# A graph attention layer on one core: one-hots 64 wide in two column groups, next terms copied by ScalarE, scores in two parts

## The chip, the core and the metric

The kernel runs on one core of a Trainium2 chip. The metric is the device time of one execution in microseconds (us). Engines are named as in the profile: PE is TensorE, DVE VectorE, ACT ScalarE, POOL GpSimd, SP SyncE.

## What is computed

A graph has 3125 nodes with 768 features and 50000 edges sorted by destination. Two residual layers follow each other; the first is a graph convolution (GCN) with two products by 768 x 768 weights, the second, which alone is changed, is graph attention with 12 heads of 64 features:

```
hh  = relu(layernorm(x)).reshape(n, 12, 64)
ft  = einsum('nhd,ed->nhe', hh, W_fc)
e   = leaky_relu(a1[src] + a2[dst], 0.2)          # a1, a2: ft times attn_l, attn_r
ee  = exp(e - segment_max(e, dst)[dst])
agg = segment_sum(ee / segment_sum(ee, dst)[dst] * ft[src], dst)
x   = x + relu(einsum('nhd,ed->nhe', hh, W_res) + agg)
```

## The kernel before, in words

The GCN fills the first 1297 us of the span. The attention part starts there and is a loop over 25 tiles of 128 nodes. With this graph each tile has one visit ("quad"): the edges that end in its 128 nodes, in 16 chunks of 128 edges (4 subtiles of 32 nodes, called units 0 to 3 here, with 4 chunks each) and one shared chunk for what is left over. The last tile has 53 nodes and two units.

For each visit POOL issues 17 indirect gathers (L1243). Each brings 128 rows of 3168 B from `table3` into the ring buffer `ring`: for each head 64 features and a one, and behind them the 12 source terms a1. The ring holds two visits, so the gathers of visit q+2 for a unit wait for `used[s]` of visit q, which PE sets after that unit's products.

DVE builds `hot` (L1555), a bf16 one-hot of each edge's node within its subtile, and ACT casts it to fp32 as `hot_f` (L1344, `cast_hot`). PE transposes `hot` (L1442), ACT copies that out (L1330), and PE makes the scores of the next visit in PSUM (`scores`, L1447): four products from the transposed one-hots (L1454 to L1457), and then five that add the source terms of the gathered rows (L1461). The terms come from the ring by two DVE copies (L1561, L1562, `take_terms`), which wait until all gathers of that visit have landed.

Then ACT makes the leaky part (L1336, `sloped`), DVE takes a running maximum in both directions along the edges (L1613 to L1619) and subtracts it (L1621), PE transposes the result (L1471), and ACT takes the exponentials (L1368 for DVE's units, L1372 for unit 3). DVE multiplies the gathered rows of units 0, 1 and 2 in place with the weights (L1650) and the shared chunk (L1657); ACT does unit 3 in 48 small operations (L1388). PE adds up the weighted rows (L1492; shared chunk L1507): for every chunk four products, one for each column group g of 32 columns. Each has as weights the 32-wide one-hot of the chunk's subtile and streams the 195 columns of three heads. Sums of head group g lie in partitions 32g to 32g+31 of `ps_acc`, with the subtile in the free dimension.

DVE divides the sums by their denominators (L1567 to L1573, `divide`) into `o_g`, and ACT (`lay`, L1354) moves `o_g` into node order in `ps_n` in 16 copies of 32 x 192. PE adds the residual product to it (L1419, `natural`), and DVE finishes the tile (L1579, `finish`), which SP stores (L1277). `divide` of tile j-1, `lay` of j-1 and `finish` of j-2 run in the visit of tile j.

Each engine works through its list in program order. On ACT it is: cast of the one-hots, exponentials, copy of the transposed one-hots, `a2_of`, 48 scalings, `sloped`, `lay`. On PE: transposes of the exponents' scores, transposes of `hot`, `natural`, a small start of the sums (L1483), units 0 to 2, all scores of the next visit, the shared chunk, unit 3. On DVE: units 0 to 2, `take_terms`, shared chunk, `finish`, the one-hot for two visits ahead, the maximum chain, `divide`. `rescale` runs only where a tile has a second visit; no row of the trace comes from it.

## Time and profile before

| | before |
|---|---|
| median of 3 runs | 1899.82 us (1897.61 to 1903.91) |
| profiled execution | 1901.22 us, its span 1899.5 us |
| granted PE clock, mean | 0.881 of full speed |
| PE / PEld / DVE / ACT / POOL busy | 1327.0 / 879.2 / 1123.7 / 716.8 / 1234.5 us |
| 1672.73 to 1694.97, one visit: PE / DVE / ACT / POOL busy | 15.98 / 18.98 / 19.92 / 16.83 us |
| in that visit: clock, DMA share, GB/s | 0.81, 0.97, 350 |

The profiled execution is 1.7 us longer than its span. Busy shares are read for the attention part alone, since only it is changed. PEclk is the granted clock: 1.00 is 2.4 GHz, 0.50 is 1.2 GHz.

### The profile page before, as it was taken

To read this page: it belongs to the slowest core of one execution; us is meant where nothing else is said; L and a number is where in the kernel's file an instruction comes from. 1 tells how busy PE (TensorE), PEld (TensorE's weight loads), DVE (VectorE), ACT (ScalarE), POOL (GpSimd) and SP (SyncE) were. 2 spreads that over 40 slices of the span, in tenths; PEclk is the share of its full clock that TensorE was granted. 3 is DMA by queue.
4 is the path that set the end of the run, shared out by engine and by line. 5 is a ranking of instruction groups with operands and counts; after the bars stand their busy time and mean duration, and the time that the engine had idled before them with its cause. 6 is when DMAs were issued, how large, how long until landed. Compare 5 with 4: busy or idle time off the path is not lost. (4 is left out here: it accounts for less than half of the span.)

```text
span 1899.5 us, 43588 instructions
## 1 busy us (share of the span) xinstructions
PE 1327.0 (70%) x13579; PEld 879.2 (46%) x13580; DVE 1123.7 (59%) x2027; ACT 716.8 (38%) x2184; POOL 1234.5 (65%) x1297
## 2 busy tenths in 40 slices
PE   6426877787877847777777777793566676677665
PEld 6314444444544524444444444492344544444453
DVE  6623454444544525545555555562788888888887
ACT  6600111111111100001000010171688998989885
POOL 3137777777777457777777777204777777777760
PEclk9977898989999978899999899997788878888887
DMA  6589999999999679999999999388999999999992
GB/s 219 208 210 361 331 328 336 333 332 331 335 334 330 230 239 334 330 324 329 323 333 334 330 326 331 140 322 291 314 335 347 348 352 347 345 347 343 357 320 69
DMA packets 139991, 585.22 MB, mean 308 GB/s; under 512 B 30615, under 2 KB 32751, under 8 KB 139945
## 3 DMA queue, kind: packets, MB, share of 16 engines
q0 software_dynamic: 100272, 497.49, 74.3%
q1 hardware_dynamic: 32563, 67.72, 10.1%
q10 hardware_dynamic: 7110, 19.43, 2.9%
q8 instruction: 25, 0.41, 0.1%
q14 instruction: 21, 0.17, 0.0%
HBM read 534.42 MB, written 50.12 MB: 308 GB/s over the span
## 5 line engine op out<-in xcount | busy, mean ns | idle before, releaser
L667 POOL DMA_INDIRECT ring_c<-table,slot_c x834 | 797.0, 956 | 313.6 <-issue 293.9
L1243 POOL DMA_INDIRECT ring<-table,slot x417 | 413.3, 991 | 141.5 <-issue 115.9
L711 ACT ACTIVATE slot_c<-units 128x8 int32 (+1 forms) x104 | 21.7, 210 | 857.9 <-DMA ring_c<-table,slot_c 812.0
L1388 ACT ACTIVATE ring<-ring,weight x1152 | 279.0, 335 | 0.6
L833 DVE TENSOR_TENSOR hots<-iota,units 128x256 f32<-128x256 bf16 x102 | 43.5, 428 | 391.3 <-PE ps_sum0a L779 123.0
L1650 DVE TENSOR_TENSOR ring<-ring,ps_w 128x3120 f32 x72 | 242.7, 3398 | 16.8 <-ACT ps_w L1368 16.5
L1492 PE MATMUL ps_acc<-ring,hot_f 128*32 128x195 f32 x3136 | 179.1, 376 | 86.0 <-DVE ring L1650 84.1
L808 PE MATMUL ps_ya<-weights,sum_ta 128*128 128x512 f32 (+1 forms) x576 | 190.9, 488 | 0.0
L808 PE MATMUL ps_yb<-weights,sum_tb 128*128 128x512 f32 (+1 forms) x576 | 189.7, 486 | 0.0
L1492 PEld LDWEIGHTS ps_acc<-ring,hot_f 128*32 128x32 f32 x3136 | 105.1, 124 | 148.1 <-DVE ring L1650 109.3
L808 PEld LDWEIGHTS ps_ya<-weights,sum_ta 128*128 128x128 f32 x576 | 110.2, 191 | 77.3 <-issue 69.6
L808 PEld LDWEIGHTS ps_yb<-weights,sum_tb 128*128 128x128 f32 x576 | 109.5, 190 | 76.4 <-issue 68.9
L779 PE MATMUL ps_sum0a<-ring_c,hots 128*32 128x192 f32 x1600 | 86.4, 368 | 78.5 <-DMA ring_c<-table,slot_c 78.5
L779 PE MATMUL ps_sum0b<-ring_c,hots 128*32 128x192 f32 x1600 | 84.9, 361 | 70.0 <-DMA ring_c<-table,slot_c 70.0
L779 PE MATMUL ps_sum1b<-ring_c,hots 128*32 128x192 f32 x1536 | 85.5, 373 | 64.2 <-DMA ring_c<-table,slot_c 64.2
L779 PE MATMUL ps_sum1a<-ring_c,hots 128*32 128x192 f32 x1536 | 85.7, 373 | 62.4 <-DMA ring_c<-table,slot_c 62.4
L1354 ACT ACTIVATE ps_n<-o_g 32x192 f32<-32x192 f32 x384 | 124.6, 324 | 7.7 <-DVE nodes L1579 3.6
L779 PEld LDWEIGHTS ps_sum0a<-ring_c,hots 128*32 128x32 f32 x1600 | 57.9, 121 | 104.8 <-issue 75.0
L779 PEld LDWEIGHTS ps_sum0b<-ring_c,hots 128*32 128x32 f32 x1600 | 57.5, 118 | 95.5 <-issue 79.9
L779 PEld LDWEIGHTS ps_sum1b<-ring_c,hots 128*32 128x32 f32 x1536 | 57.0, 122 | 90.5 <-issue 77.3
L779 PEld LDWEIGHTS ps_sum1a<-ring_c,hots 128*32 128x32 f32 x1536 | 56.9, 122 | 88.7 <-issue 79.2
L854 DVE TENSOR_TENSOR ps_sum0a<-ps_sum0a,naturala 32x192 f32<-32x192 f32 x200 | 73.3, 367 | 8.3 <-ACT naturala L739 5.7
(294 smaller groups left out, 1940.2 us busy)
## 6 DMA issues: line engine op xcount, KB each, us to landing
ring_c<-table,slot_c POOLq DMA_INDIRECT x834, 5.4
table<-ft SPq DMA_DIRECT2D x25, 396.0 KB, 2.8
table<-nodes SPq DMA_DIRECT2D x25, 384.0 KB, 3.3
table<-nodes ACTq DMA_DIRECT2D x25, 384.0 KB, 5.3
turned_table<-h_t SPq DMA_DIRECT2D x25, 384.0 KB, 3.0
nodes<-in_x ACTq DMA_DIRECT2D x24, 384.0 KB
turned_g<-turned_table SPq DMA_DIRECT2D x24, 384.0 KB, 6.5
out_x<-nodes SPq DMA_DIRECT2D x24, 384.0 KB
```

Source lines behind the costliest of these rows:

```text
L667: eng.indirect_dma_start(out=ring[:, t * QH + k, :], out_offset=None, in_=table, in_offset=bass.IndirectOffsetOnAxis(ap=slot[t][:, k:k + 1 ...
L711: eng.activation(slot[t][:, :], units[:, ds(q, 1), t * QH:(t + 1) * QH + t].rearrange("p a c -> p (a c)"), ACT.Copy).then_inc(slot_ready[t ...
L779: last = eng.matmul(block_of(par, s, g), hot, rows[:, g * GB:(g + 1) * GB], start=start, stop=True, skip_group_check=True)
L808: last = eng.matmul(product(jj)[:, c0:c0 + n], turned(jj)[:, k, :], w[:, k, c0:c0 + n], start=(k == 0), stop=(k == KB - 1))
L833: eng.tensor_tensor(hots[k][:, :, :].rearrange("p (s c) d -> p s c d", c=CPU), iota0[:, :].unsqueeze(1).unsqueeze(2).to_broadcast([P, 2, C ...
L854: last = eng.tensor_tensor(block_, block_, natural[s * UD:(s + 1) * UD, g * GB:(g + 1) * GB], ALU.add)
L1243: eng.indirect_dma_start(out=ring[:, b * RB + at * FROW:b * RB + (at + 1) * FROW], out_offset=None, in_=table3, in_offset=bass.IndirectOff ...
L1354: last = eng.activation(ps_n[s * UD:(s + 1) * UD, c0:c0 + GN], o[g * UD:(g + 1) * UD, s, :], ACT.Copy)
L1388: last = eng.activation(head, head, ACT.Copy, scale=weight[:, c, h:h + 1])
L1492: last = eng.matmul(acc_of(s, g), hot_f[:, c, s * UD:(s + 1) * UD], ring[:, x0 + g * GW:x0 + (g + 1) * GW], start=False, stop=True, skip_g ...
L1650: eng.tensor_tensor(mine, mine, given_w[:, 0:CPU, s * H:(s + 1) * H].unsqueeze(3).to_broadcast([P, CPU, H, FH]), ALU.mult).then_inc(scaled ...
```

## The change

The four column groups of 32 become two of 64 (`GA = 2`, `AW = 64`). The fp32 one-hot `hot_f` now holds for every chunk three blocks of 32 columns: the subtile's one-hot, a block of zeros that is set once, and the one-hot of its neighbour. `hot_of(s, c)` takes two adjacent blocks, so that a subtile's one-hot stands in the lower or the upper half of 64 columns, with zeros in the other. A chunk now has two products that stream 390 columns of six heads, where it had four of 195. The shared chunk uses `hot_x`, which is 128 wide with no zero half: four products of 390 columns where there were 16 of 195. `ps_acc` takes two whole banks for two half tiles.

`cast_hot` becomes three copies, and stands behind the exponentials. `lay` becomes four copies of 64 x 384. The closing additions of the last tile become two of 64 rows where there were eight of 32. `take_terms` moves from DVE to ACT, where it stands in front of the last 12 of the 48 scalings (and in front of `lay` in the last tile). `scores` is split: the four products of the one-hots come after unit 1, the five of the terms after unit 2. The sizes of `rden`, `lifts`, `head_of` and `o_g` follow.

```diff
+GA = 2
+UA = US // GA
+AW = UA * UD
-            hot_f = sb(st, "hot_f", [P, UC, P])
+            hot_f = sb(st, "hot_f", [P, GA, CPU, 3, UD])
+            hot_x = sb(st, "hot_x", [P, P])
-            def acc_of(s, g):
-                return ps_acc[g * UD:(g + 1) * UD, s * 256:s * 256 + GW]
+            def acc_of(t, g):
+                return ps_acc[g * AW:(g + 1) * AW, t * 512:t * 512 + GW]
+            def hot_of(s, c):
+                return hot_f[:, s // UA, c, s % UA:s % UA + 2, :].rearrange("p x d -> p (x d)")
+                    def take_terms(q):
+                        rows_landed(eng, q, bounds, passed)
+                        given = ring[:, ds(eng.snap(eng.snap(q % 2) * RB), RB)].rearrange("p (c f) -> p c f", f=FROW)[:, :, H * FH:FROW]
+                        eng.activation(terms[:, 0:CPU, :].rearrange("p c (s h) -> p s c h", h=H), given[:, 0:QX, :].rearrange("p (s c) h -> p s c h", c=CPU), ACT.Copy)
+                        eng.activation(terms[:, CPU, :].rearrange("p (s h) -> p s h", h=H), given[:, QX:QC, :].to_broadcast([P, US, H]), ACT.Copy).then_inc(terms_in, 1)
                     def cast_hot(q, j):
...
-                        eng.activation(hot_f[:, :, :].rearrange("p c e -> p (c e)"), hot[:, ds(par, 1), :, :].rearrange("p a c e -> p (a c e)"), ACT.Copy).then_inc(hot_cast, 1)
+                        given = hot[:, ds(par, 1), :, :]
+                        for t in range(GA):
+                            eng.activation(hot_f[:, t, :, 0:3:2, :], given[:, :, 0:CPU, t * AW:(t + 1) * AW].rearrange("p a c (s d) -> p (a c) s d", d=UD), ACT.Copy)
+                        eng.activation(hot_x[:, :], given[:, :, CPU, :].rearrange("p a e -> p (a e)"), ACT.Copy).then_inc(hot_cast, 1)
                     def lay(j):
...
-                        for g in range(US):
-                            for s in range(US):
-                                c0 = g // 2 * 512 + g % 2 * GN
-                                last = eng.activation(ps_n[s * UD:(s + 1) * UD, c0:c0 + GN], o[g * UD:(g + 1) * UD, s, :], ACT.Copy)
+                        for g in range(GA):
+                            for t in range(GA):
+                                last = eng.activation(ps_n[t * AW:(t + 1) * AW, g * 512:g * 512 + GN], o[g * AW:(g + 1) * AW, t, :], ACT.Copy)
                         def follow(q, nth, left):
-                            cast_hot(q, j)
...
                                 eng.activation(weight[:, :, :], ps_e[:, 0:CPU, mine * H:(mine + 1) * H], ACT.Exp).then_inc(own_made, 1)
+                            cast_hot(q, j)
                             turn_hot(q + 1)
...
+                                if c == CPU - 2:
+                                    take_terms(q + 1)
...
-                                    for g in range(US):
-                                        last = eng.matmul(acc_of(s, g), hot_f[:, c, s * UD:(s + 1) * UD], ring[:, x0 + g * GW:x0 + (g + 1) * GW],
+                                    for g in range(GA):
+                                        last = eng.matmul(acc_of(s // UA, g), hot_of(s, c), ring[:, x0 + g * GW:x0 + (g + 1) * GW],
                                                           start=False, stop=True, skip_group_check=True)
...
-                                for s in range(nu):
-                                    for g in range(US):
-                                        last = eng.matmul(acc_of(s, g), hot_f[:, CPU, s * UD:(s + 1) * UD], ring[:, x0 + g * GW:x0 + (g + 1) * GW],
+                                for t in range(-(-nu // UA)):
+                                    for g in range(GA):
+                                        last = eng.matmul(acc_of(t, g), hot_x[:, t * AW:(t + 1) * AW], ring[:, x0 + g * GW:x0 + (g + 1) * GW],
...
                             by_parity(eng, eng.snap(q % 2), first_products)
-                            scores(q + 1)
+                            scores_of_hots(q + 1)
+                            if early_of(j) > 2:
+                                by_parity(eng, eng.snap(q % 2), next_products)
+                            scores_of_terms(q + 1)
                             by_parity(eng, eng.snap(q % 2), other_products)
...
-                                if s == early_of(j) - 1:
-                                    take_terms(q + 1)
...
-                    for g in range(US):
-                        for s in range(LU):
-                            r, c0 = slice(s * UD, (s + 1) * UD), g // 2 * 512 + g % 2 * GN
-                            last = eng.tensor_tensor(ps_s[r, c0:c0 + GN], ps_s[r, c0:c0 + GN], o[g * UD:(g + 1) * UD, s, :], ALU.add)
+                    for g in range(GA):
+                        r, c0 = slice(0, LU * UD), g * 512
+                        last = eng.tensor_tensor(ps_s[r, c0:c0 + GN], ps_s[r, c0:c0 + GN], o[g * AW:g * AW + LU * UD, 0, :], ALU.add)
```

`first_products` is now units 0 and 1, `next_products` unit 2.

## Rows read from the trace of the kernel before

**Rows 1.** Waits of POOL, 1300 to 1870: waiter, releaser, us, times, longest.
```profile
POOL ring L1243 <- issue: 115.9, 371, 0.6
POOL ring L1243 <- PE ps_acc L1492: 13.5, 32, 2.6
```

**Rows 2.** Chain that ended last, one visit: start, us, what.
```profile
1682.93 1.53 PE ps_acc L1492 x32
...
1685.25 0.86 PE ps_s L1457 x2
1686.11 1.11 PE ps_s L1461 x10
...
1687.84 0.31 ACT ps_n L1354
...
1693.63 0.16 ACT hot_f L1344
...
1694.39 0.36 ACT ps_w L1368
...
1694.97 0.12 DVE ring L1650
```

**Rows 3.** Timeline of the same visit: start, us, engine, line, what, idle before.
```profile
1672.73 3.40 DVE L1650 TENSOR_TENSOR ring<-ring,ps_w 128x3120 f32 x1 [0.70 <-ACT ps_w L1368]
...
1676.19 2.83 PE L1492 MATMUL ps_acc<-ring,hot_f 128*32 128x195 f32 x32 [0.84 <-DVE ring L1650]
...
1679.62 2.37 PE L1492 MATMUL ps_acc<-ring,hot_f 128*32 128x195 f32 x32 [0.60 <-DVE ring L1650]
...
1682.93 1.53 PE L1492 MATMUL ps_acc<-ring,hot_f 128*32 128x195 f32 x32 [0.94 <-DVE ring L1650]
...
1683.76 0.26 DVE L1561 COPY terms<-ring 128x192 f32 x1 [0.88 <-DMA ring<-table,slot]
...
1687.13 1.53 PE L1507 MATMUL ps_acc<-ring,hot_f 128*32 128x195 f32 x32
1687.24 0.70 ACT L1336 ACTIVATE top_g<-ps_s 48x640 f32<-48x640 f32 x1 [1.63 <-PE ps_s L1461]
...
1687.84 5.37 ACT L1354 ACTIVATE ps_n<-o_g 32x192 f32<-32x192 f32 x16
...
1692.09 0.82 DVE L1621 TENSOR_TENSOR score<-ps_s,top_g 48x640 f32<-48x640 f32 x1
...
1693.31 0.96 DVE L1573 TENSOR_TENSOR o_g<-ps_acc,rden 128x768 f32<-128x768 f32 x1
```

**Rows 4.** Groups of the second half by form: count, busy us, mean ns.
```profile
L1561 DVE COPY terms<-ring 128x192 f32 x25 | 6.6, 264 | 17.2 <-DMA ring<-table,slot 15.8 <-issue 1.4
...
L1372 ACT ACTIVATE weight<-ps_s 128x48 f32<-128x48 f32 x24 | 4.9, 206 | 0.0
```

**Rows 5.** Stretches: length, PE, PEld, DVE, ACT, POOL busy, PEclk, DMA, GB/s.
```profile
1667.80:1670.80 3.00, 0.00 (x0) 0.01 (x1) 2.90 (x5) 2.90 (x10) 2.48 (x2) 1.00 1.04 425
1672.40:1675.30 2.90, 2.88 (x14) 2.81 (x14) 2.57 (x1) 2.84 (x13) 2.29 (x3) 0.50 1.03 382
1676.19:1679.02 2.83, 2.83 (x32) 1.38 (x32) 2.83 (x2) 2.83 (x13) 2.22 (x3) 0.50 0.99 355
1679.62:1681.20 1.58, 1.58 (x20) 0.99 (x24) 1.58 (x1) 1.58 (x8) 1.03 (x2) 0.50 0.98 353
...
1587.07:1588.57 1.50, 1.50 (x32) 0.94 (x32) 1.50 (x2) 1.50 (x8) 1.20 (x2) 1.00 1.00 365
...
327.30:341.00 13.70, 7.09 (x132) 4.91 (x132) 3.62 (x6) 0.42 (x2) 10.35 (x12) 1.00 0.94 347
```

**Rows 6.** Timeline of POOL, the first gather of the next visit but one.
```profile
1679.87 0.94 POOL L1243 DMA_INDIRECT ring<-table,slot  x1 [0.53 <-issue]
```

**Rows 7.** Timeline of the tail.
```profile
1881.55 1.53 PE L1492 MATMUL ps_acc<-ring,hot_f 128*32 128x195 f32 x32 [0.37 <-DVE ring L1636]
...
1886.17 2.96 DVE L1678 TENSOR_TENSOR ps_s<-ps_s,o_g 32x192 f32<-32x192 f32 x8 [0.57 <-PE ps_s L1527]
```

More of the change, by code:

```diff
@@ L1234, in _ @@
                     eng.wait_ge(g_mask, 1)
-                    for g in range(US):
-                        last = eng.affine_select(out=head_of[:, g, :, :], in_=head_of[:, g, :, :], compare_op=ALU.not_equal, fill=1.0, base=-g * PR,
-                                                 pattern=[[-H, US], [-1, PR]], channel_multiplier=1)
+                    for g in range(GA):
+                        for s in range(UA):
+                            last = eng.affine_select(out=head_of[:, g, s, :, :], in_=head_of[:, g, s, :, :], compare_op=ALU.not_equal, fill=1.0, base=-s * H - g * PR,
+                                                     pattern=[[-UA * H, GA], [-1, PR]], channel_multiplier=1)
                     last.then_inc(g_const, 1)
@@ L1432, in rescale @@
                         eng.sem_inc(passed, 1)
-                        for g in range(US):
-                            last = eng.matmul(ps_l[g * UD:(g + 1) * UD, 64:64 + US * PR], lift[:, :], head_of[:, g, :, :].rearrange("p s k -> p (s k)"), start=True, stop=True)
+                        for g in range(GA):
+                            for s in range(UA):
+                                r0 = g * AW + s * UD
+                                last = eng.matmul(ps_l[r0:r0 + UD, 64:64 + GA * PR], lift[:, :], head_of[:, g, s, :, :].rearrange("p t k -> p (t k)"), start=True, stop=True)
                         last.then_inc(r_all, 1)
@@ L1443, in turn_hot, with scores_of_hots @@
                         last.then_inc(hot_tr, 1)
-                    def scores(q):
+                    def scores_of_hots(q):
                         eng.wait_ge(hot_tc, q + 1)
@@ L1481, in visit @@
                                     eng.sem_inc(passed, 1)
-                                for s in range(0, US, 2):
-                                    eng.matmul(ps_acc[:, s * 256:s * 256 + 2], ident_b[:, :], nil[:, :], start=True, stop=True, skip_group_check=True)
+                                for t in range(GA):
+                                    eng.matmul(ps_acc[:, t * 512:t * 512 + 2], ident_b[:, :], nil[:, :], start=True, stop=True, skip_group_check=True)
                             with eng.Else():
@@ L1496, in first_products, with next_products @@
                             def first_products(b):
-                                for s in range(early_of(j)):
+                                for s in range(min(2, early_of(j))):
+                                    unit(b, s)
+                            def next_products(b):
+                                for s in range(2, early_of(j)):
                                     unit(b, s)
@@ L1504, in other_products @@
                                 x0 = b * RB + QX * FROW
-                                for s in range(nu):
-                                    for g in range(US):
-                                        last = eng.matmul(acc_of(s, g), hot_f[:, CPU, s * UD:(s + 1) * UD], ring[:, x0 + g * GW:x0 + (g + 1) * GW],
+                                for t in range(-(-nu // UA)):
+                                    for g in range(GA):
+                                        last = eng.matmul(acc_of(t, g), hot_x[:, t * AW:(t + 1) * AW], ring[:, x0 + g * GW:x0 + (g + 1) * GW],
                                                           start=False, stop=True, skip_group_check=True)
@@ L1517, in _ @@
                     turn_hot(0, 0)
-                    scores(0)
+                    scores_of_hots(0)
+                    scores_of_terms(0)
                     tiles(eng, step)
@@ L1674, in _ @@
                     eng.wait_ge(o_nat, NT)
-                    for g in range(US):
-                        for s in range(LU):
-                            r, c0 = slice(s * UD, (s + 1) * UD), g // 2 * 512 + g % 2 * GN
-                            last = eng.tensor_tensor(ps_s[r, c0:c0 + GN], ps_s[r, c0:c0 + GN], o[g * UD:(g + 1) * UD, s, :], ALU.add)
+                    for g in range(GA):
+                        r, c0 = slice(0, LU * UD), g * 512
+                        last = eng.tensor_tensor(ps_s[r, c0:c0 + GN], ps_s[r, c0:c0 + GN], o[g * AW:g * AW + LU * UD, 0, :], ALU.add)
                     last.then_inc(o_den, 1)
                     eng.wait_ge(o_den, NT * 2 + 1)
-                    mine = node(NT - 1)[0:LAST].rearrange("p (g x) -> p g x", g=2)
-                    eng.scalar_tensor_tensor(out=mine, in0=ps_s[0:LAST, :].rearrange("p (g x) -> p g x", g=2)[:, :, 0:2 * GN], scalar=0.0, in1=mine, op0=ALU.max, op1=ALU.add).then_inc(o_fin, 1)
+                    mine = node(NT - 1)[0:LAST].rearrange("p (g x) -> p g x", g=GA)
+                    eng.scalar_tensor_tensor(out=mine, in0=ps_s[0:LAST, :].rearrange("p (g x) -> p g x", g=GA)[:, :, 0:GN], scalar=0.0, in1=mine, op0=ALU.max, op1=ALU.add).then_inc(o_fin, 1)
 def kernel(**inputs):
```

44 lines of the change are left out of this document (20 added, 24 removed).

## The prediction

> **What bounds the kernel now.** I read the waits of POOL first, because the DMA share is 0.97 in the attention part and the gathers could be the bound. Nearly all its gaps are the 0.31 us between two issues (115.9 us in 371) [rows 1]. A gather takes 0.95 us, so 17 need 17 x (0.95 + 0.30) = 21.25 us. In each visit one or two gathers are longer, together by some 0.75 us, which makes 22.0; visits follow each other at 22.2. The first gather of a visit starts 0.85 us after PE has ended unit 0 (1679.02 [rows 3], the gather at 1679.87 [rows 6]), with a gap of 0.53 where 0.30 is usual. So POOL is nearly full, and waits 0.2 us per visit for unit 0's products.
>
> Second, the chain of waits over one visit [rows 2]. It runs from unit 2's products (1682.93) over the scores (to 1687.2) and ACT's `lay` to the cast (1693.63), the exponentials (1694.39) and the next L1650 (1694.97). The timeline of the same visit [rows 3] gives the other branch: the maximum chain ends with L1621 at 1692.91 and PE's transposes of it at 1693.5. Both branches meet at the cast. All times below are counted from DVE's start on unit 0, 1672.73. The next one is at 22.24. PE does unit 0 from 3.46 to 6.29, unit 1 from 6.89, unit 2 from 10.20 to 11.73, and the terms' products end at 14.47.
>
> Third, stretches with the granted clock [rows 5]. PE is idle for 3.0 us before the transposes, the clock falls to 0.50, and `natural` and unit 0 run at half speed. Of the 25 first stretches of unit 0, 17 are at 0.50, 7 at 1.00 (1587.07 is one), one is between.
>
> **The change part by part.**
>
> *Products, the added cost.* At the full clock 10 records of 128 columns (five fp32 products) take 1.11 us, two of 512 columns take 0.86 [rows 2]: time goes by columns, four passes at 2.4 GHz (5 x 128 x 4 / 2400 = 1.07; 512 x 4 / 2400 = 0.85), not by records. A unit has 16 products of 195 columns and takes 1.53 us [rows 3]. One after another they would take 16 x 195 x 4 / 2400 = 5.2; over four groups at once 1.30, and 0.2 for the end of the pipe. So four groups do run at once. After the change a unit has 8 products of 390 columns over two groups: 8 x 390 x 4 / 2400 / 2 = 2.6 us, 1.3 more. If two groups of 64 did not overlap it would be 5.2, and if records were what costs, 0.8. The 1.53 us row fits overlap to 0.2 us and the 0.86 row excludes cost by records, so I take 2.6, with 2.7 where the next start counts. That is 5.2 us more PE work per visit. The shared chunk stays at 4 x 390 x 4 / 2400 / 2 = 1.3, near the 1.53 of now. PE goes from 15.98 us busy to about 21 of 22.2, so its slack is gone.
>
> The Trainium skill (TensorE: Matmul & The Clock Gate, "Measured speedup vs the span model") gives 2.38 for three column tiles at once. The trace has 5.2 / 1.53 = 3.4 for four, which is the better measure here.
>
> *Order of the scores.* The four products of the one-hots take 1.65 us (1684.46 to 1686.11 [rows 2]), 1.5 without the start. Now they come after unit 2; then they stand between units 1 and 2, where PE is idle for 1.7 us before unit 2. That would save 1.5 us, but the longer unit 1 eats it. At the full clock: unit 0 from 3.46 to 6.1, unit 1 from 6.89 to 9.6, one-hots to 11.1, unit 2 to 13.8, terms to 14.95. That is 0.5 us later than 14.47. At half clock: unit 0's 2.6 us of work begins at half speed. In the visit shown the clock was still 0.50 five us after unit 0 began (1681.20 [rows 5]) and rose there, since unit 1 took 2.37 and unit 2 took 1.53 [rows 3]; in the visit before it had risen after 3.4. I take 4.3 us at half speed, which does 2.15 of the work: unit 0 ends at 3.46 + 4.3 + 0.45 = 8.2. Then unit 1 to 10.9, one-hots 12.4, unit 2 15.1, terms 16.2: 1.7 us later than now. With 5.2 us at half speed it is 2.2 later.
>
> *Cast behind the exponentials.* The exponentials start 0.76 us earlier, at 20.9 instead of 21.66 (1693.63 to 1694.39 [rows 2]). DVE must also have finished `divide`, which ends at 1694.27 [rows 3], 0.70 before L1650 starts. So 0.65 us of it are gained. The cast now takes three copies. From 0.206 us for 48 elements [rows 4] and 0.74 for 640, an element costs 0.9 ns and a copy 0.16 us to begin: 2 x 0.39 + 0.28 = 1.06 us. It ends about 1 us into the visit, 2.4 before PE's first product: hidden.
>
> *`lay`.* Now 16 x 0.335 = 5.37 us on the chain [rows 2, 3]. Four copies of 384 elements cost 4 x (0.16 + 0.35) = 2.0. The 3.3 us gained do not shorten the visit, since the maximum chain of DVE ends at the same moment (1692.91, transposes to 1693.5). After `lay` goes, that branch alone is left.
>
> *Terms.* DVE loses 0.26 + 0.18 us and a wait of 0.88 for landing [rows 3]. It is idle afterwards until `sloped`, so that is worth nothing. ACT gains two copies of 192 and 48 elements, 0.33 + 0.21 us, and the wait. ACT starts its 48 scalings about 1.1 us later (the cast), reaches the terms at some 11.1 and ends at 14.5. If POOL is later by unit 0's delay, the rows land at some 12.5, which pushes the end of the scalings to 16: behind it is `sloped`, which PE's terms let start at 15.0 to 16.2. So the cover is thin but holds. If it is gone, ACT adds up to 0.5 us. SP's load of the next slots and POOL's queue get nothing new in front of them; `finish` and its store come 0.5 to 1 us earlier.
>
> *Sum.* Full clock: -0.65 + 0.5 = -0.15 per visit, 22.1 us, just over POOL's 22.0. Half clock: -0.65 + 1.7 = +1.05, 23.3 us. Now 17 of 25 visits start unit 0 at half clock. PE's idle time before the transposes shrinks from 3.0 to about 2 us (unit 3 ends at z + 4.0, transposes begin at z + 6, z the end of the terms), so somewhat fewer should: I take 0.65. Then 0.65 x 1.05 - 0.35 x 0.15 = +0.63, over 24 steps from visit to visit +15 us. Head: nothing, everything before the first rows land is covered. Tail: unit 1's products 1.53 become 2.7, the closing eight additions 2.96 [rows 7] become two of 384 elements, 0.96 for 768 elements gives about 0.55 each, so -1.85; with an order of products on PE that is up to 1 later, about 0. Profiled execution: 1901.2 + 15 = 1916; it was 1.4 above the median of the runs, so 1915.
>
> **The rivals.**
>
> *A. The clock holds.* Every visit costs -0.15, or at POOL's pace -0.2: 1899.8 - 4 = 1896. For it: in the GCN, bursts of 1.5 us with gaps of up to 2.4 us keep the clock at 1.00 (327.30 to 341.00 [rows 5]), and the new gap is 2 us. Against: the transposes did not keep it up before, and with them the stretch without products is 3.4 us. The Trainium skill (same page, "HAM oscillation — how this bites in real kernels") has it that short enough gaps between bursts leave the clock up, which is this rival.
>
> *B. PE's work was not what mattered, faster.* If a unit costs no more than now, the one-hots' products hidden and the cast gone give -2 us for the engines, and POOL is left: 22.0, or 21.25 if its long gathers vanish. That is -0.2 to -1.0 x 24 = -5 to -23, middle 1886. The column rates speak against it.
>
> *C. Locked at half clock, slower.* The longer visit makes every unit 0 begin at half speed, and the clock rises late: +1.05 to +1.55 x 24 = +25 to +37, 1931. It decides when the share of half-clock visits goes from 17 in 25 to all.
>
> *D. Groups of 64 do not overlap.* 2.6 us more for each unit: terms end some 8 us later, +7.5 x 24 = +180, 2080. Nothing in the trace shows two groups of 64, so it can't be excluded.
>
> **How the numbers follow.** Forecast 0.50; A 0.20; B 0.10; C 0.17; D 0.03. Differences under 0.3% (5.7 us) are not told from no change. The forecast's own range is 1903 to 1927 (share of half-clock visits 0.35 to 1.0), of which a tenth falls within 0.3%. A is within 0.3% for three quarters and faster for the rest; B is faster but for a fifth. Faster: 0.05 + 0.09 = 0.14, say 0.15. Same: 0.05 + 0.15 + 0.02 = 0.22. Slower: 0.63. The range leaves out most of B and D and the top of C: 1892 to 1935.
>
> **What would show it.** Right: a unit's products at 2.6 to 2.8 us at the full clock (16 records); no `lay` and no cast in the chain of waits, in their place the products of units 1 and 2; `sloped` starting at 15 to 16.3 after L1650's first start instead of 14.5; L1368 right behind the transposes of L1471; visits 22.1 us apart where unit 0 starts at the full clock and 23.3 where not; gaps of POOL before the first gather that grow to 1 us and more. Wrong: a unit of 1.5 us (B) or 5.2 (D), a clock that never falls (A), or an ACT that ends its scalings after PE's terms in every visit.

## The result, and the profile after

The median is 1907.94 us (7 runs, 1901.69 to 1913.67) against 1902.96 us of the kernel before beside it (7 runs, 1897.61 to 1904.87). The ratio is 1.0038, 95% interval 1.0020 to 1.0055: slower by 4 to 10 us, where the sum had +15. The profiled execution took 1913.67 us, the longest of the seven, with a span of 1911.9.

I cut both profiled executions at the same three events. The attention part begins with POOL's first `head_of` instruction; then the first scaling of a unit 0 (L1650 before, L1674 after), the last one 24 visits later, and the end.

| us | before | after | difference |
|---|---|---|---|
| up to the attention part (GCN, unchanged) | 1296.45 | 1299.79 | +3.3, scatter |
| from there to the first unit 0 | 39.72 | 43.29 | **+3.6** |
| 24 visits | 536.49 (22.35 each) | 542.13 (22.59 each) | **+5.6** |
| from the last unit 0 to the end | 26.84 | 26.69 | -0.15 |

The groups of the second half, with line, engine, operation, tile, count | busy, mean ns | idle before and its releasers, to hold beside [rows 2 to 4, 7]:

```profile
L1515 PE MATMUL ps_acc<-ring,hot_f 128*64 128x390 f32 x1568 | 315.8, 521 | 25.8 <-DVE ring L1674 24.4 <-ACT ring L1404 0.6 <-DVE ring L1661 0.3
...
L1369 ACT ACTIVATE ps_n<-o_g 64x384 f32<-64x384 f32 x96 | 46.6, 486 | 2.7 <-DVE nodes L1604 1.8
...
L1348 ACT ACTIVATE terms<-ring 128x192 f32 x25 | 9.0, 362 | 21.9 <-DMA ring<-table,slot 21.1 <-issue 0.8
```

A visit that begins at the full clock, as a timeline (start, us, engine, line, what, idle before). It is 21.89 long:

```profile
1753.18 3.40 DVE L1674 TENSOR_TENSOR ring<-ring,ps_w 128x3120 f32 x1
...
1756.63 2.84 PE L1515 MATMUL ps_acc<-ring,hot_f 128*64 128x390 f32 x16 [1.31 <-DVE ring L1674]
...
1764.64 0.36 ACT L1348 ACTIVATE terms<-ring 128x192 f32 x1 [0.51 <-DMA ring<-table,slot]
...
1766.86 1.15 PE L1484 MATMUL ps_s<-ident,terms 128*48 128x128 f32 x9
...
1768.15 0.70 ACT L1343 ACTIVATE top_g<-ps_s 48x640 f32<-48x640 f32 x1
1768.75 1.98 ACT L1369 ACTIVATE ps_n<-o_g 64x384 f32<-64x384 f32 x4
...
1773.97 0.48 PE L1494 MATMUL ps_s<-ident,score 48*128 48x48 f32 x5 [1.92 <-DVE score L1646]
...
1775.07 3.40 DVE L1674 TENSOR_TENSOR ring<-ring,ps_w 128x3120 f32 x1
```

A unit takes 2.84 us. `sloped` (L1343) starts 14.97 after unit 0's scaling, where it was 14.51. PE's gap before the transposes (L1494) is 1.92, where it was 3.0 [rows 5].

The next two visits show what the mean hides, first one whose unit 0 began at half clock (L1515 at 1664.70), then the one after it, at the full clock:

```profile
1661.25 3.40 DVE L1674 TENSOR_TENSOR ring<-ring,ps_w 128x3120 f32 x1
...
1664.70 7.86 PE L1515 MATMUL ps_acc<-ring,hot_f 128*64 128x390 f32 x32 [0.78 <-DVE ring L1674]
...
1670.77 0.94 POOL L1250 DMA_INDIRECT ring<-table,slot  x1 [2.12 <-PE ps_acc L1515]
...
1677.83 0.70 ACT L1343 ACTIVATE top_g<-ps_s 48x640 f32<-48x640 f32 x1 [1.88 <-PE ps_s L1484]
...
1684.74 3.40 DVE L1674 TENSOR_TENSOR ring<-ring,ps_w 128x3120 f32 x1
...
1698.75 0.36 ACT L1348 ACTIVATE terms<-ring 128x192 f32 x1 [3.06 <-DMA ring<-table,slot]
1699.15 2.97 ACT L1404 ACTIVATE ring<-ring,weight  x12
...
1699.39 1.15 PE L1484 MATMUL ps_s<-ident,terms 128*48 128x128 f32 x9 [0.79 <-ACT terms L1349]
...
1702.02 0.68 ACT L1343 ACTIVATE top_g<-ps_s 48x640 f32<-48x640 f32 x1
```

The first is 23.49 long: PE is late, so POOL stands 2.12 us before it may refill unit 0. The second is longer still, 24.43. Its rows land 3 us late, ACT takes the terms only at 14.0 of the visit, and `sloped` waits for the 12 scalings behind them although PE's products had ended at 1700.65 (nine records are shown, the tenth runs from 1700.38). It starts at 17.3. The chain of waits over the same stretch says it in its own way (start, us, what): PE, then POOL and the landing, and no `lay` and no cast anywhere.

```profile
1664.70 7.86 PE ps_acc L1515 x32
...
1688.20 2.87 PE ps_acc L1515 x16
1691.19 0.94 POOL ring L1250
1692.43 5.75 DMA ring<-table,slot
```

The waits of POOL for the units' products, to hold beside [rows 1], have doubled:

```profile
POOL ring L1250 <- PE ps_acc L1515: 26.9, 44, 5.1
```

The longest, 5.1 us, is the one before the loop's first refill of unit 0 (at 1352.83), behind the late head; in the loop itself they reach 2.1.

Three stretches of after (length; busy of PE, PEld, DVE, ACT, POOL; granted clock; DMA share; GB/s): the first 1.5 us of unit 0 in the half-clock visit and in the full-clock visit shown, and 450 us of visits.

```profile
1664.71:1666.21 1.50, 1.50 (x6) 0.67 (x8) 1.50 (x2) 1.50 (x8) 1.14 (x2) 0.50 1.02 356
1756.64:1758.14 1.50, 1.50 (x10) 0.76 (x12) 1.50 (x2) 1.50 (x8) 1.15 (x2) 1.00 1.08 369
1400.00:1850.00 450.00, 377.12 (x2282) 230.08 (x2280) 371.04 (x301) 346.37 (x1302) 338.51 (x341) 0.92 0.96 346
```

Of 25 such starts nine are at 0.50 or 0.55 (17 at 0.50 before [rows 5]), seven between 0.69 and 0.90, nine at 1.00. Counted from 21.9, the nine low visits are 8.9 us too long together. The visits that follow them are 7.1 too long (1.31, 1.94, 1.14, 2.53, 0.21), and another one 0.53. Then 24 x 21.9 + 8.9 + 7.7 = 542. This split belongs to one execution, and experiment 1 shows how far it scatters.

### The profile page after: what moved, and what is told of

Read it like the earlier page. It is cut to its first block and busy times, and to the rows that moved or that the text cites. A ratio compares the mean times of both kernels' runs of the same rounds, so it can differ in the third digit from the quotient of the medians.

```text
span 1911.9 us, 39119 instructions
## 1 busy us (share of the span) xinstructions
PE 1421.7 (74%) x11423; PEld 902.4 (47%) x11424; DVE 1111.1 (58%) x1970; ACT 655.0 (34%) x1998; POOL 1240.2 (65%) x1297
## 5 line engine op out<-in xcount | busy, mean ns | idle before, releaser
L1515 PE MATMUL ps_acc<-ring,hot_f 128*64 128x390 f32 x1568 | 315.8, 521 | 25.8 <-DVE ring L1674 24.4
L1674 DVE TENSOR_TENSOR ring<-ring,ps_w 128x3120 f32 x72 | 242.6, 3398 | 1.9 <-ACT ps_w L1382 1.9
L1515 PEld LDWEIGHTS ps_acc<-ring,hot_f 128*64 128x64 f32 x1568 | 143.5, 145 | 160.1 <-issue 99.6
L856 DVE TENSOR_TENSOR ps_sum0b<-ps_sum0b,naturalb 32x192 f32<-32x192 f32 x200 | 73.3, 367 | 7.9 <-ACT naturalb L741 5.3
```

The lines of the kernel that those rows point to most:

```text
L856: last = eng.tensor_tensor(block_, block_, natural[s * UD:(s + 1) * UD, g * GB:(g + 1) * GB], ALU.add)
L1515: last = eng.matmul(acc_of(s // UA, g), hot_of(s, c), ring[:, x0 + g * GW:x0 + (g + 1) * GW], start=False, stop=True, skip_group_check=True)
L1674: eng.tensor_tensor(mine, mine, given_w[:, 0:CPU, s * H:(s + 1) * H].unsqueeze(3).to_broadcast([P, CPU, H, FH]), ALU.mult).then_inc(scaled ...
```

## The experiments

Four theories were open: ACT takes the first terms in front of the work that PE waits for (head); DVE's or ACT's order makes the late landing count twice (late visits); the half clock is what starts the late visits; and products of 2.8 us leave PE so full that anything more on it is paid for.

**1. ACT's order in the head alone.**

```
                         tile_quads(eng, j, follow)
-                    take_terms(0)
                     turn_hot(0)
                     a2_of(0)
+                    take_terms(0)
```

> The changed kernel, with the very first copy of the terms on ACT put behind the first copy of the transposed one-hots and a2_of, where the changed kernel has it in front. Theory T: in the trace of the changed kernel the scores of the first visit start only after the rows have landed, so the first L1650 comes 3.6 us later after the start of the attention part than before. This run gives that back: 39.7 us instead of 43.3 from the part's first instruction to the first scaling, and 3.6 us less in time than the changed kernel (some 1904 where that has 1908). Rival R1: all of the loss is in the loop (PE's longer products), and this moves less than 1 us.

Measured: 1904.64 (12 runs) against 1903.36, ratio 1.0006 (0.9989 to 1.0024). From the start of the part to the first unit 0 it is 40.15 instead of 43.29; the 24 visits take 538.9 (after 542.1). The timeline of after's head:

```profile
1329.22 0.36 ACT L1348 ACTIVATE terms<-ring 128x192 f32<-128x192 f32 x1 [32.50 <-DMA ring<-table,slot]
1329.62 0.68 ACT L1337 ACTIVATE hot_t<-ps_s 128x640 f32<-128x640 bf16 x1
...
1331.16 0.63 PE L1475 MATMUL ps_s<-hot_t,a_blk 128*48 128x128 f32 x2 [23.92 <-ACT a_blk L1332]
...
1335.90 0.70 ACT L1343 ACTIVATE top_g<-ps_s 48x640 f32<-48x640 f32 x1 [4.84 <-PE ps_s L1484]
```

and of this kernel's:

```profile
1302.83 0.63 PE L1475 MATMUL ps_s<-hot_t,a_blk 128*48 128x128 f32 x2 [1.65 <-ACT a_blk L1332]
...
1323.67 0.36 ACT L1348 ACTIVATE terms<-ring 128x192 f32<-128x192 f32 x1 [20.95 <-DMA ring<-table,slot]
...
1326.69 0.70 ACT L1343 ACTIVATE top_g<-ps_s 48x640 f32<-48x640 f32 x1 [2.52 <-PE ps_s L1484]
```

In after the copy of the transposed one-hots stands behind a wait of 32.5 us for the first rows, so PE's scores of the one-hots begin only at 1331. Without that they are done 20 us before the rows land. From the terms to `sloped` it is 3.0 us instead of 6.7. The head is shown.

The loop of this kernel is that of after, line for line, so its profile also says how much one execution differs from another: 12 of 25 units begin at 0.50 (after: 9 at 0.50 or 0.55), these visits are 10.4 us too long together, the ones behind them only 2.8 (after: 8.9 and 7.1), and the longest wait of POOL for a unit is 2.1 us.

**2. The terms back on DVE**, as the last work before its maximum chain (the two copies as in the kernel before, behind `next_hot`), the rest as after:

```
-                                if c == CPU - 2:
-                                    take_terms(q + 1)
...
                             eng.wait_ge(hot_cast, q + 1)
                             next_hot(q + 2)
+                            take_terms(q + 1)
```

> The changed kernel with the terms' copies back on DVE, but behind the one-hot of two visits ahead, where DVE is idle. Theory T: in the changed kernel six or seven visits end late (sloped 15.2 to 17.3 us after the first scaling instead of 15.0) because the terms landed late and 12 of ACT's scalings stand between the terms and sloped, 3.4 us from the terms' start to sloped. With DVE the terms' start is followed by sloped 0.5 + 1.2 us later at the earliest. Expected: the head gives 3.6 us back as well, visits after one with a half clock cost up to 1.6 us less each, some 6 in all; 10 us less than the changed kernel, 1898, ratio to before 0.998. Rival R1 (only PE's products and the clock set the visits): nothing in the loop, 3.6 us in the head alone, 1904. Rival R2 (POOL's pace is the bound): visits of 22.0, nothing in the loop either where the clock was full.

Measured: 1904.25 (12 runs), ratio 1.0006 (0.9991 to 1.0021). The head is 39.82; that half of the expectation came. The visits take 544.7, no less than after: the half on the late visits failed. The timeline shows who holds `sloped` now:

```profile
1639.96 0.28 DVE L1583 COPY terms<-ring 128x192 f32 x1 [0.84 <-DMA ring<-table,slot]
...
1642.81 0.70 ACT L1343 ACTIVATE top_g<-ps_s 48x640 f32<-48x640 f32 x1 [2.47 <-DVEq L1629]
```

`sloped` needs two signals: PE's products (the last record ended at 1641.7) and one that DVE's queue gives when it enters the next turn of its loop (L1629), behind the copies of the terms. DVE's last copy ended at 1640.3 and the signal came 2.5 us later. So the late terms now hold `sloped` through DVE's queue instead of ACT's scalings, and nothing was won. ACT's order is not the cause by itself: at the two places tried, late terms cost the same.

**3. PE kept busy in its gap**: after, with eight products of 128 columns into an unused part of PSUM at each visit's end.

```
                             by_parity(eng, eng.snap(q % 2), other_products)
+                            for _ in range(8):
+                                eng.matmul(ps_l[:, 128:256], wres_b[:, :], wres_b[:, :], start=True, stop=True, skip_group_check=True)
...
+                    eng.wait_ge(wres_in, 48)
```

> The changed kernel with eight more products of 128 x 128 (fp32, into an unused part of a PSUM bank) at the end of each visit on PE, in the idle time ahead of the transposes: 1.7 us of work in a gap of 1.9. Theory T: visits that start unit 0 at half clock, and those behind them, make up all of the loop's loss. With the clock kept at 1.00 every visit takes 21.9 us: 24 x 21.9 = 526 us from the first to the last scaling of unit 0, instead of 542; 16 us less than the changed kernel, 1892. Rival R3: the clock is a symptom, the late visits come from the landing of rows (DMA is at 0.97) and stay: 540 us. Rival R4: the products in the gap delay the transposes, and each visit gets up to 0.5 us longer.

Measured: 1911.47 (11 runs), ratio 1.0042 (1.0029 to 1.0055); visits 540.0 (22.50 each). A stretch like those above, and the filler with the transposes behind it:

```profile
1707.38:1708.88 1.50, 1.50 (x10) 0.76 (x12) 1.50 (x2) 1.50 (x8) 1.17 (x2) 1.00 1.08 313
```

```profile
1722.72 2.05 PE L1547 MATMUL ps_l<-wres_b 128*128 128x128 f32 x16
...
1725.22 0.48 PE L1494 MATMUL ps_s<-ident,score 48*128 48x48 f32 x5 [0.45 <-issue]
```

Unit 0 starts at 1.00 in 22 of 25 visits. The twenty visits from the fourth on have `sloped` at 14.98 or 14.99 and a length of 22.36 to 22.44. ACT's waits for the rows, 1400 to 1850, tell the same, after first and then this kernel:

```profile
ACT terms L1348 <- DMA ring<-table,slot: 17.7, 16, 3.1
```

```profile
ACT terms L1348 <- DMA ring<-table,slot: 2.6, 3, 1.7
```

So where the half clock is gone, the late visits are gone. Two things changed at once, though: a visit of 22.4 us also leaves POOL, which needs about 21.9 to 22.0 for its 17 gathers, some 0.4 us of room in each. What shows the link by itself are the waits in after: POOL stands 2.05 and 2.12 us in the half-clock visits that begin at 1480.45 and 1661.25, and the terms of the next visits wait 2.46 and 3.06 us for their rows. How much the room contributed is not shown. The filler itself costs 0.5 us of each visit, because it ends at 1724.77 and DVE had the scores ready at 1724.57 (`<-issue`, not `<-DVE`): what the clock gave back, the filler took. At this place PE has no room for eight more products.

**4. The groups of 64 without the new order** (the short `lay` and the cast in three copies come with them): after with the cast in front of the exponentials, the scores whole behind unit 2, and the terms on DVE as before. In short:

```
                         def follow(q, nth, left):
+                            cast_hot(q, j)
...
-                            scores_of_hots(q + 1)
                             if early_of(j) > 2:
                                 by_parity(eng, eng.snap(q % 2), next_products)
+                            scores_of_hots(q + 1)
                             scores_of_terms(q + 1)
```

> One part of the change alone: two column groups of 64 with the zero half, the short lay, the three copies of the cast; but the cast in front of the exponentials, the scores in one piece behind unit 2, and the terms on DVE behind unit 2, as before. Theory T: units of 2.8 us make the terms' products end at 3.46 + 2.8 ... : unit 2 from 10.2 to 13.0, scores 2.7 more: 15.6 instead of 14.5 at full clock, 16.5 at half. The cast falls into the time that lay has left, so it costs nothing in front: visits of 22.24 - 0.65 + 1.1 = 22.7 at full clock, 23.5 at half; +0.8 x 24 = +19 us on before, 1922. Rival R5 (lay was what bounded the visits and the products cost nothing): 22.0 per visit, 1897. Rival R6 (the split of the scores is worth nothing because PE's idle time was there anyway): same time as the changed kernel, 1908.

Measured: 1916.34 (6 runs), ratio 1.0061 (1.0041 to 1.0081); visits 550.9 (22.95 each), one at the full clock 22.59 with `sloped` at 15.67 (forecast 22.7 and 15.6). Against before the groups of 64 with their short `lay` cost 14 us in the visits. ACT's part behind `sloped` in that visit:

```profile
1561.74 0.70 ACT L1343 ACTIVATE top_g<-ps_s 48x640 f32<-48x640 f32 x1 [2.66 <-PE ps_s L1474]
...
1565.83 0.72 ACT L1353 ACTIVATE hot_f<-hot 128x256 f32 x2 [1.50 <-PE ps_acc L1505]
...
1568.07 0.35 ACT L1377 ACTIVATE ps_w<-ps_s 128x240 f32<-128x240 f32 x1 [1.32 <-PE ps_s L1484]
```

The cast is done at 1566.74, before the maximum chain has ended, so it costs nothing although it stands in front. From `sloped` to the exponentials it is 6.33 us, exactly what it is in after (1768.15 to 1774.48), and 7.15 in the kernel before (1687.24 to 1694.39). With the short `lay` the place of the cast makes no difference. In experiment 5, with the long `lay` and the cast behind, it is 6.62, and 0.25 of that is transposes at half clock. So either edit alone takes nearly all of the 0.82 us, and both together no more.

**5. The order alone**: the kernel before, with the cast behind the exponentials and the scores in two parts; groups of 32, `lay` and terms untouched.

```
                         def follow(q, nth, left):
-                            cast_hot(q, j)
...
                                 eng.activation(weight[:, :, :], ps_e[:, 0:CPU, mine * H:(mine + 1) * H], ACT.Exp).then_inc(own_made, 1)
+                            cast_hot(q, j)
...
-                                for s in range(early_of(j)):
+                                for s in range(min(2, early_of(j))):
                                     unit(b, s)
...
-                            scores(q + 1)
+                            scores_of_hots(q + 1)
+                            if early_of(j) > 2:
+                                by_parity(eng, eng.snap(q % 2), next_products)
+                            scores_of_terms(q + 1)
```

> The kernel before with the cast behind the exponentials and the scores in two parts, four column groups of 32, once more, since the last two calls ran where gathers moved 270 GB/s. If the gathers run at 345 GB/s, Theory T: with units of 1.5 us the one-hots' products fit into PE's idle time, sloped starts at 13.0 instead of 14.5, POOL and the landing of rows set the visits: 21.3 to 21.9, loop 515 to 526 instead of 536, ratio to before 0.991 to 0.995. Rival R2: POOL's pace is 22.0, ratio 0.997. Rival R7: lay (5.37 us behind sloped) still holds the exponentials, so only the 0.65 of the cast and the 1.5 of the scores count, which POOL again cuts. If the gathers are slow: 0.996 to 1.0 as in the two calls before.

Measured: **1892.13** (9 runs, 1888.68 to 1897.17) against 1901.88, ratio **0.9954** (0.9942 to 0.9967): faster than both kernels. One visit of it:

```profile
1687.95 3.40 DVE L1660 TENSOR_TENSOR ring<-ring,ps_w 128x3120 f32 x1 [0.16 <-ACT ps_w L1367]
...
1696.99 1.02 PE L1457 MATMUL ps_s<-hot_t,a_blk 128*48 128x512 f32 x2
1698.15 1.53 PE L1494 MATMUL ps_acc<-ring,hot_f 128*32 128x195 f32 x32
...
1699.19 0.26 DVE L1571 COPY terms<-ring 128x192 f32 x1 [1.10 <-DMA ring<-table,slot]
...
1699.70 1.26 PE L1463 MATMUL ps_s<-ident,terms 128*48 128x128 f32 x10
...
1702.60 0.70 ACT L1336 ACTIVATE top_g<-ps_s 48x640 f32<-48x640 f32 x1 [1.00 <-DVEq L1617]
...
1708.41 0.73 PE L1473 MATMUL ps_s<-ident,score 48*128 48x48 f32 x5 [4.67 <-DVE score L1631]
...
1709.80 3.40 DVE L1660 TENSOR_TENSOR ring<-ring,ps_w 128x3120 f32 x1 [0.17 <-ACT ps_w L1367]
```

and POOL's waits over its attention part, to hold beside [rows 1]:

```profile
POOL ring L1243 <- issue: 114.2, 375, 0.3
POOL ring L1243 <- PE ps_acc L1494: 11.8, 30, 1.6
```

A visit takes 21.85 here and 22.03 in the mean (528.7 for 24). DVE waits 0.16 where it waited 0.70 [rows 3]. PE had the terms' scores ready at 1700.96, and `sloped` starts 1.6 later: DVE still has the shared chunk, `finish` and the next one-hot in front of its signal, to 1702.04, and began them late by the landing (1.10). `sloped` waits for that signal in 21 of the visits. Over 20 visits the pace is 22.01, the 22.0 that the prediction gave POOL, and nearly all of POOL's gaps are the 0.3 us of an issue: what is left is the pace of the gathers, and DVE's order behind the landing. The pace is no fixed number: over the four visits of after from 1753.18 to 1840.76 POOL has no gap over 0.31 us and needs 21.9, with one long gather in each.

The clock is not as the prediction had it. PE's gap before the transposes is 4.67 us, longer than the 3.07 of before, and the transposes themselves run at half clock (0.73 us instead of 0.48). Yet only 9 of 25 units 0 begin at 0.50, five lie between 0.57 and 0.69, five between 0.81 and 0.93, six are at 1.00. The length of that gap alone does not set the share.

The runs below were made where the gathers of the unchanged GCN moved less. The record numbers the chips: experiments 1 to 4 ran on chip 8 and experiment 5 on chip 5, but 6, 7, 9 and 10 on chip 0, and 8, 11 and 12 on chip 11. One row each, 100 to 600 us, of the kernel before at the usual rate and of experiment 6:

```profile
100.00:600.00 500.00, 360.86 (x3405) 219.16 (x3406) 214.45 (x517) 63.21 (x111) 362.52 (x382) 0.89 0.94 325
```

```profile
100.00:600.00 500.00, 374.33 (x2769) 198.65 (x2770) 171.29 (x412) 49.12 (x88) 298.11 (x315) 0.82 0.82 271
```

The kernel before takes 2288.59 us beside experiments 6, 7, 9 and 10, 2313.15 beside 8 and 11, and 2289.46 beside 12. They are another regime, and it is not one of late rows: from 1600 to 1860 the terms of experiment 6 never wait for a landing. There PE's own products start late, with gaps that nothing in the profile explains:

```profile
PE ps_acc L1492 <- issue: 49.9, 81, 1.8
```

In the kernel before at the usual rate PE has no such wait for these products in the same stretch. POOL waits for PE, so the gathers slow down with it. These runs say how the orders stand in that regime, not what they do at the usual rate.

**6. The cast alone** on the kernel before, and **7, 8. the order alone** (the kernel of 5), there:

```
-                            cast_hot(q, j)
                             with eng.If(nth < 1):
                                 eng.sem_inc(r_exp, 1)
...
                                 eng.activation(weight[:, :, :], ps_e[:, 0:CPU, mine * H:(mine + 1) * H], ACT.Exp).then_inc(own_made, 1)
+                            cast_hot(q, j)
                             turn_hot(q + 1)
```

> The kernel before with the one-hots' cast behind the exponentials, nothing else. Theory T: the cast gives back up to 0.65 us of the 22.24 in front of L1650; POOL then is the next bound. In the changed kernel stretches of visits follow each other at 21.90 with no wait of POOL, so POOL's pace is at most that: visits of 21.6 to 21.9, loop 520 to 528 instead of 536, ratio 0.995. Rival R2 (POOL's pace is 22.0 to 22.2 and the gain is lost there): loop 530 and more, ratio 0.998 to 1.0, POOL waits vanish. Rival R7: lay, which keeps its 5.37 us, ends with the maximum chain and keeps the exponentials where they were: no gain at all.

> The kernel before with the cast behind the exponentials and the scores in two parts (after unit 1 and after unit 2), with four column groups of 32 and all else as before. Theory T: with units of 1.5 us PE's idle time between units 1 and 2 does hold the one-hots' products, the terms' products end at 13.0 instead of 14.5 and the engines alone would need 20.1 to 20.7 us a visit; so POOL's pace or the landing of the rows sets the visits: 21.3 to 21.9, loop 515 to 526, ratio 0.991 to 0.995. Rival R2: POOL's pace is 22.0: same as the run with the cast alone.

> The kernel before with the cast behind the exponentials and the scores in two parts, four column groups of 32: again, for the same reason. If the gathers run at 345 GB/s: Theory T: the engines' loop is 20.1 to 20.7 us, POOL and the landing of rows set the visits: 21.3 to 21.9, loop 515 to 526, ratio 0.991 to 0.995. Rival R2: POOL's pace is 22.0 and nothing is gained over 0.997. If the gathers are slow again: 0.996 as there.

Measured: the cast alone 2286.02 (12 runs), 0.9994 (0.9980 to 1.0007); the order 2279.40 (10 runs), 0.9958 (0.9945 to 0.9971), and beside 2313.15 it is 2311.49 (12 runs), 0.9985 (0.9970 to 0.9999). So the order is ahead in all three comparisons, by 0.4 to 0.5% in two and by 0.15% in the third, where the interval almost reaches 1. That the cast alone is worth nothing there does not say what it is worth at the usual rate; this stays open.

**9. DVE's scalings of units 1 and 2 left out**, to see POOL's own pace:

```
+                                if s > 0:
+                                    eng.tensor_copy(rows[:, s * CPU, 0, :], rows[:, s * CPU, 0, :]).then_inc(scaled[s], 1)
```

> The kernel before, with DVE's scaling of units 1 and 2 left out (one small copy in its place), so the weights of these two units are missing from the result. The engines' loop gets 6.7 us shorter, and the visits show the pace of POOL and the DMA alone. Theory T: 17 gathers of 1.25 us and 0.3 to 0.8 us of longer ones: 21.5 to 21.9 us a visit. Rival R2: 22.0 or more. If nothing but the issue counts: 21.3.

Measured: one run, 2298.28 beside 2288.59; visits of 28 to 30 us. Inconclusive: where a visit is that long, 22.0 can't be seen. Kernel 5 answered it.

**10 to 12. Experiment 1 with a filler of five products** instead of eight:

```
+                            for _ in range(5):
+                                eng.matmul(ps_l[:, 128:256], wres_b[:, :], wres_b[:, :], start=True, stop=True, skip_group_check=True)
```

> The changed kernel with five instead of eight products of 128 x 128 in PE's gap at the end of a visit (1.3 us, where eight took 2.05 and pushed the transposes 0.5 us back), and with the first copy of the terms behind a2_of. Theory T: the clock stays at 1.00 and nothing is pushed: 21.9 a visit from the fourth on, loop 527 to 530 instead of 542, the head 3.6 us shorter: 1889 to 1893 where the changed kernel has 1908, ratio to before 0.994. Rival R8: 1.3 us of work is too little to keep the clock, visits at half clock come back: 1900 and more. Rival R2: at full clock POOL holds the visits at 22.0 to 22.2: 1896.

> The same kernel as the last one, again, because in the call before the kernel before itself took 2289 us, with gathers that moved 270 instead of 345 GB/s. If the gathers run at 345 GB/s: Theory T as before: the clock stays at 1.00, visits of 21.9, loop 527 to 530, ratio to before 0.994. Rival R8: the clock is not kept, 1900 and more. Rival R2: POOL at 22.0 to 22.2, ratio 0.997. If the gathers are slow again: PE's later end of unit 0 stands in the loop from a row's use to the next gather, so about 1.02 as there.

> The changed kernel with five products of 128 x 128 in PE's gap at the end of a visit and the first copy of the terms behind a2_of, once more, where gathers run at 345 GB/s if the last call's do. Theory T: eight of them kept sloped at 14.98 in all visits but cost 0.5 us each; five (1.3 us) leave the transposes alone: visits of 21.9 to 22.0 (POOL's pace was 22.0 in the last run), loop 528 to 531 instead of 542, and the head 3.6 us shorter: ratio to before 0.995. Rival R8: 1.3 us is too little to keep the clock; some visits of 22.4 to 24 remain, ratio 1.000 as with the first terms moved alone.

Measured, each time where gathers are slower: 2343.03 (6 runs), 1.0243 (1.0213 to 1.0273); 2380.76 (6 runs), 1.0264 (1.0225 to 1.0304); 2361.05 (4 runs), 1.0305 (1.0263 to 1.0346). The 64-wide products with a filler cost 2.4 to 3% there. POOL's waits in the first of them, 1300 to 1880:

```profile
POOL ring L1250 <- PE ps_acc L1515: 70.3, 13, 11.7
```

The rows are not late here either: from 1600 to 1860 ACT never waits for them before it takes the terms (10.0 us in after). PE is: the five filler products, 1.3 us by the expectation, are spread from 1691.87 to 1698.73 in one visit, with gaps `<- issue` of up to 2.5 us. How much of the loss is the filler's and how much the wide groups' was not separated, and whether five products pay at the usual rate stays open.

## Why the prediction was right

The edits of the change come apart as a square of four kernels, by the length of the 24 visits in the profiled execution:

| us for 24 visits | groups of 32 | groups of 64 |
|---|---|---|
| cast first, scores whole, terms on DVE | 536.5 (before) | 550.9 (4) |
| cast behind, scores split | 528.7 (5, terms on DVE) | 542.1 (after), 544.7 (2, terms on DVE) |

By rows the wide groups cost 14.4 us in the old order and 13.5 in the new one (16.0 where the terms are on DVE in both); by columns the new order gains 7.8 with groups of 32 and 8.8 with groups of 64 (6.2 with the terms on DVE). Each cell is one execution, and the same loop gave 542.1 and 538.9 in two of them, so differences of 3 us are not told apart. The ratios of the times say the same: 1.0061 for the groups in the old order, 0.9954 for the order alone. What is left of the two together is small: with the head mended (experiment 1) the ratio to before is 1.0006, 0.9989 to 1.0024, no difference. The direction of the prediction therefore hangs on the head as well.

*The number: right in part by luck.* Counted from a visit of 22.24 us, the sum and the profile compare like this:

| us | forecast | measured |
|---|---|---|
| full-clock gain, 24 visits | 24 x -0.15 = -3.6 | 24 x (21.9 - 22.24) = -8.2 |
| half clock, above a full-clock visit | 0.65 x 24 x 1.2 = +18.7 | +8.9 |
| late visits | 0 | +7.7 |
| irregular visits of before itself | 0 | 24 x 22.24 - 536.5 = -2.7 |
| head | 0 | +3.6 |
| tail | 0 | -0.15 |
| together | +15 | +9 |

Without the two terms that the prediction put at nothing, late visits and head, this gives -2 us, which would not have been told from no change. The half clock was costed at twice what it took, and that covered for both. So the range was met by errors that partly cancel; the mechanisms below are right one by one only where it says so.

*Products: right.* Forecast 2.6 to 2.7 us for a unit, measured 2.84. Two groups of 64 do overlap, so rival D falls; time goes by columns, so B falls.

The Trainium skill (TensorE: Matmul & The Clock Gate, "Measured speedup vs the span model") gives 2.38 for three tiles at once. By 8 products of 390 columns in four passes at 2.4 GHz, 5.2 us one after another, two groups gain 5.2 / 2.84 = 1.83; the 3.4 of four groups stands in the prediction.

*Order of the scores and the cast: right at the full clock.* `sloped` at 14.97 to 14.98, forecast 14.95. The visit is 21.9, forecast 22.1. The sum gave only 0.15 of the two edits' gain after the wider units; 0.34 came: `sloped` is 0.47 later, and the stretch behind it 0.82 shorter where the cast had been given 0.65. With groups of 32 it came down to POOL's pace, 22.0.

*`lay`: price right, role wrong.* Four copies take 1.98 (forecast 2.0), and in after nothing more is gained from them, since DVE's maximum chain holds the transposes until 1773.97. But the prediction let both branches meet at the cast. The cast does not wait for the maximum chain, as experiment 4 shows, where it runs while the chain is still at work; in the kernel before the cast came late because ACT was at `lay` until 1693.2. So what was put down to the moved cast could be had by the short `lay` alone.

*Half clock: mechanism right, share mis-sized.* In the visit shown `sloped` starts at 16.6 (forecast 16.2) and the visit takes 23.5 (forecast 23.3). Over the nine such visits the mean is 22.9. But the share is 9 of 25, 0.36, where I took 0.65. This is the term that made the sum too large. PE's gap before the transposes went from 3.07 to 1.92, as forecast, but that this is why the share fell is not shown: kernel 5 has 9 of 25 as well, with a gap of 4.67, and experiment 1, with 1.92, has 12. Rival A ("the clock holds") is half true, C did not come.

The Trainium skill (the same page, "HAM oscillation — how this bites in real kernels") has it that long enough gaps in PE's work between bursts bring the clock down. Experiment 3 agrees: with 2.05 us of products in the gap, 22 of 25 units begin at 1.00.

*Late visits: a term that I did not have.* The prediction named the growing waits of POOL (1.0 to 2.1 us measured) and then cost only the visit in which they stand. The rows that they delay are the next visit's, and that one is up to 2.5 us longer although PE is at the full clock: 7.1 us in all here, 2.8 in the same loop of experiment 1. "The cover is thin but holds", with up to 0.5 us if it does not, failed here: `sloped` is held for 1.4 us behind ACT's scalings (PE done at 1700.65, `sloped` at 1702.02).

*Head: the step that failed.* "Nothing, everything before the first rows land is covered" counted what the change makes PE and ACT do, not the order in which ACT does it. A wait for a landing was put in front of two short copies that PE needs, and the work that used to be hidden in front of the landing now stands behind it: 3.6 us, experiment 1 takes back 3.1.

*Tail: right*, -0.15 for about 0. (In experiments 2 to 4 the tail is 28.4 to 28.9 us instead of 26.7; this was not followed up.)

Together: I had +15 for the visits and 0 for the head; it is +5.6 and +3.6, and the rest of the profiled execution's +12.4 lies ahead of the attention part, in code that did not change. The ratio over all runs, +4 to +10 us, agrees with 9.

The version to keep is kernel 5, 0.46% faster than before: the order without the wide groups. With wide groups, the head mended (experiment 1) only brings the kernel back to even.

## What to carry to other kernels

Before a wait for a transfer is moved to another engine, list what stands behind it in that engine's order at the start of the loop as well as in the middle, where nothing hides it. Half as many matmuls with twice the columns over half as many column groups take nearly twice the time (2.84 us against 1.53); count columns per group, not instructions. When one visit is late in releasing a ring buffer, the bill comes one visit later, so cost the pair. When a forecast is met, compare its terms one by one before trusting it for the next change.

## What was not expected of the hardware

- The same kernel took 1902 to 1903 us in some comparisons and 2289 to 2313 in others, with 325 GB/s against 271 and 267 in the same stretch of gathers. The slow ones are those on chips 0 and 11, and PE's products stand apart there by gaps that no engine or transfer explains (49.9 us of 260 in experiment 6). Why was not found out.
- A signal that DVE's queue gives as it turns its loop came 2.5 us after its last work had ended (experiment 2, `<-DVEq`), but 0.56 us after it in experiment 5 (1702.04 to 1702.60). Busy times show neither.
- The granted clock over 1.5 us is often neither level: seven of 25 starts lie between 0.69 and 0.90, so it rose or fell in the middle of the unit's products.
